# Convolution taps as one multiply-and-add per chunk, and new instruction orders in the second layer of a fused transformer kernel

## What is computed

```python
    h = _L0_tok_ref(x, L0_tok_w, L0_tok_b, L0_tok_cls_token, L0_tok_pos, 16)
    h = jnp.concatenate([h, txt], axis=1)
    h = h + _L0_attn_ref(_layernorm(h, axis=-1), ...)
    h = h + _L0_ffn_ref(_layernorm(h, axis=-1), ...)
    h = h + _L1_attn_ref(_layernorm(h, axis=-1), ...)
    h = h + _L1_ffn_ref(_layernorm(h, axis=-1), ...)
```

```python
        h = bit_linear(x, w1)                                    # 256 -> 1024, rounded to 8 bits
        h = depthwise_conv1d(h.transpose(0, 2, 1), conv_w, conv_b)   # 3 taps along the tokens
        h = h.transpose(0, 2, 1)
        h = jax.nn.silu(h)
        return bit_linear(h, w2)                                 # 1024 -> 256
```

## Time and profile before

| | |
|---|---|
| Median of 3 runs | 844.23 us (842.24 to 848.17) |
| The profiled execution | 845.46 us |
| its span, first to last instruction | 843.6 us |
| mean granted clock of TensorE | 0.952 |
| TensorE busy | 773.1 us (92%) |
| VectorE busy | 596.0 us (71%) |
| ScalarE busy | 440.7 us (52%) |
| GpSimd busy | 379.4 us (45%) |

### The profile page before, as it was taken

The page is one execution under the profiler, slowest core; times in us unless marked ns, Lnnn a source line. Parts: engine busy times, 40 slices in busy tenths (PEclk is TensorE's granted clock), DMA queues, the critical chain, the costliest instruction groups (busy, mean ns, idle before and its releaser), DMA issues.

```text
span 843.6 us, 21269 instructions
## 1 busy us (share of the span) xinstructions
PE 773.1 (92%) x7399; PEld 715.3 (85%) x7399; DVE 596.0 (71%) x1446; ACT 440.7 (52%) x1047; POOL 379.4 (45%) x515
## 2 busy tenths in 40 slices
PE   4999999999999975699998999999999999999674
PEld 4999999999999965699997988988888888888464
DVE  0467776777777763144331468899999999999994
ACT  1444455444445432122221657777777777776552
POOL 1434545545555442222214766466666666653100
PEclk8999999999999986699998999899999999999788
DMA  5325321100000214577730000000000000000000
GB/s 174 99 65 205 61 58 17 25 9 9 8 9 15 64 41 35 160 219 216 208 104 21 10 13 10 8 16 15 16 16 15 15 15 16 14 9 8 10 12 14
DMA packets 27442, 43.30 MB, mean 51 GB/s; under 512 B 10549, under 2 KB 21722, under 8 KB 26826
## 3 DMA queue, kind: packets, MB, share of 16 engines
q1 hardware_dynamic: 17930, 33.03, 14.6%
q0 software_dynamic: 5808, 5.63, 3.0%
q10 hardware_dynamic: 3600, 3.28, 1.1%
HBM read 34.04 MB, written 7.88 MB: 50 GB/s over the span
## 4 chain that ended last, share of the span: by engine, by line
PE 56%; DVE 25%; issue 11%; DMA 4%; ACT 2%; POOL 1%; SPq 1%; DVEq 0%; ACTq 0%; POOLq 0%
PE bank_h L1533 5%; PE bank_b L1495 4%; PE bank_e L1507 4%; PE bank_d L1533 4%; PE bank_f L1507 4%; PE bank_g L1518 4%; PE bank_e L1691 3%; PE bank_c L1544 3%; PE bank_f L1691 3%; PE bank_c L1703 3%; PE bank_c L1484 2%; PE bank_d L1703 2%; DVE diff L926 2%; PE bank_a L1484 2%; DVE w L1241 2%
## 5 line engine op out<-in xcount | busy, mean ns | idle before, releaser
L484 POOL TENSOR_TENSOR qbd<-qt,consts_f 128x560 f32<-128x560 f32 x128 | 163.0, 1279 | 184.5 <-PE bank_e L1507 95.8
L633 ACT ACTIVATE pt<-bank_g 69x448 f32<-69x448 f32 x128 | 69.4, 542 | 34.7 <-PE bank_h L1518 33.3
L627 ACT ACTIVATE prob<-diff 112x345 f32<-112x345 f32 x128 | 62.0, 485 | 39.1 <-DVE diff L926 39.1
L1533 PE MATMUL bank_h<-values,pt 69*69 69x68 f32 x1024 | 76.4, 229 | 2.5 <-ACT pt L642 2.5
L1533 PEld LDWEIGHTS bank_h<-values,pt 69*69 69x69 f32 x1024 | 71.8, 146 | 3.0 <-ACT pt L633 3.0
L1533 PEld LDWEIGHTS bank_d<-values,pt 69*69 69x69 f32 x1024 | 70.5, 142 | 2.2
L1507 PEld LDWEIGHTS bank_e<-kt,qbd 128*112 128x112 f32 x640 | 71.0, 178 | 1.4
L1533 PE MATMUL bank_d<-values,pt 69*69 69x68 f32 x1024 | 71.8, 226 | 0.0
L1518 PE MATMUL bank_g<-consts_f,prob 112*69 112x112 f32 x512 | 71.5, 262 | 0.0
L1507 PEld LDWEIGHTS bank_f<-kt,qbd 128*112 128x112 f32 x640 | 71.1, 178 | 0.0
L1507 PE MATMUL bank_e<-kt,qbd 128*112 128x69 f32 x640 | 70.9, 258 | 0.0
(11 more groups left out here) (205 smaller groups left out, 1938.7 us busy)
## 6 DMA issues: line engine op xcount, KB each, us to landing
w<-in_w SPq DMA_DIRECT2D x25, 512.0 KB, 4.1
w<-in_w SPq DMA_DIRECT2D x1, 4096.0 KB, 15.0
patches<-in_patches SPq DMA_DIRECT2D x16, 222.0 KB, 2.6
expert_results<-prob ACTq DMA_DIRECT2D x25, 128.0 KB
expert_rows<-x SPq DMA_DIRECT2D x16, 138.0 KB
out<-h SPq DMA_DIRECT2D x16, 138.0 KB
f_raw<-in_f SPq DMA_DIRECT2D x2, 1024.0 KB, 7.8
wqkv<-in_wqkv SPq DMA_DIRECT2D x2, 768.0 KB
```

The source lines that it names most:

```text
L484: pool.tensor_tensor(qbd[u % 2][:], q.broadcast_to([128, NG, HPB, QG]), head_mask.unsqueeze(1).unsqueeze(3).broadcast_to([128, NG, HPB, QG ...
L627: act.activation(prob[u % 2][:], diff[u % 2][:], ACT.Exp, scale=DH ** -0.5).then_inc(S["prob_made"], 1)
L633: act.activation(pt[u % 2][:, :, 0:4, :].rearrange("t h g q -> t g h q"), banks["g"][0:T, 0:4 * SR].rearrange("t (g h q) -> t g h q", g=4, ...
L1533: ins = mm(heads_out[b][:, hd * (DH + 1):(hd + 1 + AHEAD) * (DH + 1)], pt[u % 2][:, i, :, :].rearrange("k g q -> k (g q)")[:, 0:T], values ...
```

## The change

The four VectorE operations of the outer taps become sixteen: for each chunk, add_tap multiplies hs by the channel's weight and adds yc in one scalar_tensor_tensor, in place, on 2 x 68 elements; eight in add_left, eight in add_right. left_tap, right_tap and their buffers go. The first tap now waits for all middle taps. conv_added counts to 16 for each pair instead of 2. scale_hidden, which writes hs, waits for the right taps of the previous pair.

```diff
-    a=[("turn_x", 1), ("turn_o", 3), ("turn_x2", 4), ("k", 1)],
-    b=[("project", 3), ("ffn_out", 6), ("turn_max", 5), ("v", 1)],
-    c=[("q", 1), ("hidden0", 4), ("hidden3", 4)],
-    d=[("spread2", 6), ("attend0", 2), ("spread1", 4)],
-    e=[("scores2", 2), ("hidden1", 4), ("scores0", 1)],
-    f=[("scores1", 2), ("scores3", 2), ("hidden2", 4)],
-    g=[("turn_p0", 2), ("turn_p1", 2), ("turn_p2", 2), ("turn_p3", 2)],
-    h=[("turn_p0", 2), ("turn_p1", 2), ("turn_p2", 2), ("turn_p3", 2)],
-    i=[("attend1", 3)],
+    a=[("k", 1), ("turn_x", 0), ("turn_o", 2), ("turn_x2", 3)],
+    b=[("turn_max", 5), ("v", 1), ("project", 2), ("ffn_out", 5)],
+    c=[("hidden0", 4), ("hidden3", 4), ("q", 0)],
+    d=[("spread2", 5), ("attend0", 1), ("spread1", 3)],
+    e=[("hidden1", 4), ("scores0", 1), ("scores2", 1)],
+    f=[("hidden2", 4), ("scores1", 1), ("scores3", 1)],
+    g=[("turn_p3", 2), ("turn_p0", 1), ("turn_p1", 1), ("turn_p2", 1)],
+    h=[("turn_p3", 2), ("turn_p0", 1), ("turn_p1", 1), ("turn_p2", 1)],
+    i=[("attend1", 2)],
...
-        taps = [cut(4), cut(5)]
...
-        FN = ("quant_chain quantized scale1_made diag1_made spread1_made hidden_made conv_mid left_made right_made conv_added tanh_made "
+        FN = ("quant_chain quantized scale1_made diag1_made spread1_made hidden_made conv_mid conv_added tanh_made "
...
-                act.wait_ge(F["conv_added"], 2 * (p + 1))
+                act.wait_ge(F["conv_added"], 2 * HFC * (p + 1))
...
+                wait(dve, F["conv_added"], 2 * HFC * (p - 1) + HFC + j1)
...
-            tap_weight = lambda k: conv[:, :, k:k + 1].unsqueeze(3).broadcast_to([128, HFC, 2, T - 1])
-
-            def left_tap(p):
+            def add_tap(p, j, dst, src, k):
+                dve.scalar_tensor_tensor(yc[:, j, :, dst:dst + T - 1], hs[:, j, :, src:src + T - 1], conv[:, j, k:k + 1],
+                                         yc[:, j, :, dst:dst + T - 1], ALU.mult, ALU.add).then_inc(F["conv_added"], 1)
+
+            def add_left(p):
 
                 for g, bank in enumerate(HIDDEN_BANKS):
                     dve.wait_ge(BK[bank], read_after(order, bank, f"hidden{g}", p))
-                dve.tensor_tensor(taps[0][:, :, :, 1:T], hs[:, :, :, 0:T - 1], tap_weight(0), ALU.mult).then_inc(F["left_made"], 1)
-
-            def right_tap(p):
-
-                for g, bank in enumerate(HIDDEN_BANKS):
-                    dve.wait_ge(BK[bank], read_after(order, bank, f"hidden{g}", p))
-                dve.tensor_tensor(taps[1][:, :, :, 0:T - 1], hs[:, :, :, 1:T], tap_weight(2), ALU.mult).then_inc(F["right_made"], 1)
-
-            def add_left(p):
-
-                dve.wait_ge(F["left_made"], p + 1)
                 dve.wait_ge(F["conv_mid"], HFC * (p + 1))
-                dve.tensor_tensor(yc[:, :, :, 1:T], yc[:, :, :, 1:T], taps[0][:, :, :, 1:T], ALU.add).then_inc(F["conv_added"], 1)
+                for j in range(HFC):
+                    add_tap(p, j, 1, 0, 0)
 
             def add_right(p):
 
-                dve.wait_ge(F["right_made"], p + 1)
-                dve.wait_ge(F["conv_added"], 2 * p + 1)
-                dve.tensor_tensor(yc[:, :, :, 0:T - 1], yc[:, :, :, 0:T - 1], taps[1][:, :, :, 0:T - 1],
-                                  ALU.add).then_inc(F["conv_added"], 1)
+                dve.wait_ge(F["conv_added"], 2 * HFC * p + HFC)
+                for j in range(HFC):
+                    add_tap(p, j, 0, 1, 2)
```

More of the change, by code:

```diff
@@ new lines, in body1 @@
+                if live(s, 1, PAIRS):
+                    turn_p(s - 1, 0)
+                if live(s, 2, PAIRS):
+                    project(s - 2)
+                if live(s, 1, PAIRS):
+                    scores(s - 1, 3)
+                    turn_p(s - 1, 1)
+                if live(s, 3, PAIRS):
+                    turn_quantized(s - 3)
+                if live(s, 1, PAIRS):
+                    attend(s - 1, 0)
+                    attend(s - 1, 1)
+                    turn_p(s - 1, 2)
@@ L1857 @@
+                if live(s, 5, PAIRS):
+                    ffn_out(s - 5)
+                if live(s, 3, PAIRS):
+                    spread_scale1(s - 3)
+            steps(pe, PAIRS, 5, body1)
 class Columns:
```

243 lines of the change are left out of this document (111 added, 132 removed).

## The result

| | before | after |
|---|---|---|
| Median, beside each other | 844.74 us (4 runs, 842.24 to 848.17) | 853.37 us (4 runs, 851.70 to 854.61) |
| Ratio | | 1.0098, 95% interval 1.007 to 1.0126 |
| The profiled execution, its span | 845.46 us, 843.6 us | 851.7 us, 849.9 us |
| Mean granted clock of TensorE | 0.952 | 0.956 |
| VectorE busy, instructions | 596.0 us, 1446 | 598.1 us, 1638 |

The kernel became 1% slower. The forecast was 837 us with a range of 824 to 850, so the time lies outside, on the other side of no change.

The account below looks back on a forecast made before the run. VectorE was taken to set the second layer's pace, TensorE 3% behind. Savings of 4.9 us between second and last hidden_max and 1.8 in filling took 845.46 to 838.8, or 837 against the median; range 824 to 850.

Parts of the forecast that it names:

- The taps: VectorE's outer taps: sixteen operations at 0.268 us, 4.29 a pair, replace four costing 4.81.
- Rival (c): Taps on VectorE do not overlap, so the kernel gets slower: step 21.9, total 853 us; chance 0.15.
- The step: Second layer, hidden_max to hidden_max: 21.09 becomes 20.9 us, with VectorE waiting 0.3 ahead of add_ffn.
- TensorE's largest wait: On TensorE, the largest wait was expected ahead of values or turn_max; no size given.
- Steps that I cost at nothing: Second layer's ScalarE and GpSimd: their delays were priced at zero, with 3.7 and 7.8 us of slack in 20.
- Nothing else on VectorE is added: VectorE's step: only the taps' cost changes, 21.09 - 4.81 + 4.29 = 20.6 us.
- Second to last hidden_max: Second layer, second to last pair's hidden_max: 278.5 us falls to 273.6, 4.9 less.
- Its two terms: In that stretch: VectorE work falls by 6.9 and 1.5 us; waits of 2.7 and 0.8 are added.
- Filling: Start of the second layer, around 530 to 535: a slow-clock stretch gives back 1.8 us, open from 0 to 3.5.
- Tail: Behind the last hidden_max: unchanged.
- The sum: Whole kernel: 4.9 plus 1.8, so 6.7 us less.
- Rival (b): No gain: the step stays at 21.1 us through TensorE or a late tanh, total 841 to 846; chance 0.18.

Follow-up runs that it names:

- e2: The changed kernel with GpSimd's add_bias moved behind mix; 843.06 us, ratio 0.9982 to the kernel before.
- e12: The changed kernel with GpSimd's gathers issued ahead of the last spread_query; 843.66 us, ratio 0.9968 to the kernel before.
- e7: e2 with ffn_out moved ahead of the third turn_p on TensorE's list; 843.92 us, ratio 0.9986 to the kernel before.
- e8: e7 with 20 instead of 8 idle products ahead of turn_max for the last two pairs; 844.4 us.
- e9: e2 with 20 instead of 8 idle products ahead of turn_max for the last pair alone; 843.36 us.
- e5: The kernel before with only z_unscale moved behind stats2 on VectorE's list; 848.16 us, ratio 1.0039 to the kernel before.
- e3: The kernel before, its orders kept, with the new taps in the places of add_left and add_right; 876.29 us, ratio 1.0368.

## Why the prediction was wrong, point by point

**The taps: right.** 0.268 each was forecast, 0.27 measured in all runs of eight that GpSimd doesn't interrupt; the duration of one is 355 ns on average (0.34 to 0.36 forecast):

```profile
L1201 DVE SCALAR_TENSOR_TENSOR w<-w,conv 128x136 f32<-128x136 f32 x256 | 73.2, 355 | 0.0
```

Rival (c) named the right sign and nearly the right time, 853, by a mechanism that is not there: the taps do overlap. That it came near is luck. The prediction cites the Trainium skill, page "VectorE: DVE Perf Modes", section "The DRAIN you can't avoid", for that rival; the same section adds that a next operation which is not held starts earlier, and with that the starts of 0.27 and 1.20 agree.

**The step: right but for one line of the sum.** 20.9 with 0.3 of wait ahead of add_ffn was forecast; e2 shows 20.95 with 0.29, and 0.20 ahead of row_max, which I hadn't named; e12 shows 20.94. TensorE's largest wait is ahead of turn_max in both, up to 0.8, as named. In after the step is 21.71.

**The step that failed** is the sentence "ScalarE and GpSimd have 3.7 and 7.8 us of slack in 20", under "Steps that I cost at nothing", together with "Nothing else on VectorE is added". I read GpSimd's busy share as whether it would be late, and no wait of VectorE's in the steps is for it. I didn't ask what runs beside what, so z_unscale and gate_hidden stand in the sum at their lone prices, and the runs show 1.16 us a step more for the two. The rows of before could have told me: the earlier trace rows has GpSimd at 12.15 of 20, so for six tenths of the time VectorE has GpSimd beside it, and in the same trace spread_query takes 1.86 where it starts during gate_hidden and 1.14 where it doesn't:

```profile
552.30 1.14 POOL L484 TENSOR_TENSOR qbd<-qt,consts_f 128x560 f32<-128x560 f32 x1
...
567.84 1.86 POOL L484 TENSOR_TENSOR qbd<-qt,consts_f 128x560 f32<-128x560 f32 x1 [4.48 <-ACT qt L663]
```

In before that cost nothing, since it was GpSimd that waited, and GpSimd had time. The new lists turned it round. Per line, between the kernels' whole second layers, z_unscale has 13.2 us in after and 3.4 in e2, gate_hidden 22.5 and 20.8:

```profile
L563 POOL DMA_INDIRECT base<-expert_results,yrow_i x32 | 58.4, 1825 | 13.8 <-issue 7.0 <-DMA expert_results<-prob 6.0 <-PE bank_e L1498 0.8
L572 POOL TENSOR_TENSOR h<-h,base 69x512 f32<-69x512 f32 x15 | 25.7, 1714 | 20.0 <-ACT base L822 20.0
L1222 DVE SCALAR_TENSOR_TENSOR w<-w 128x1104 f32<-128x1104 f32 x16 | 22.5, 1405 | 0.3 <-ACT w L829 0.2
L1344 DVE TENSOR_SCALAR qs<-am,f_mean 69x2 f32<-69x2 f32 x16 | 13.2, 825 | 0.0
```

(lines of after: busy us, mean ns of one, idle before; one gather had a mean of 1233 ns and one mix 1261 in before). The 1.16 a step meets 0.3 of wait for ffn_out that it hides, and a little more: 21.71 - 20.95 = 0.76 is what is left. Over the ten steps between the first and the eleventh pair that is 7.6 (217.10 less 209.51); the first pair's second eight taps, stretched too (3.58 for the eight from 523.04), add 1.3. The medians, 853.37 and 843.06, are 10.3 apart; the 1.4 that are left are not traced to a place.

**Second to last hidden_max.** Forecast 4.9 less than before, e2 has 278.52 - 274.81 = 3.7 less. Its two terms can be checked by the busy time in that stretch, 274.43 in before and 265.69 in e2. The work fell by 8.7, where 6.9 + 1.5 = 8.4 was forecast (I had multiplied 14 by 0.49, the rounded step's gain; with the taps' own 4.81 - 4.29 = 0.52 it is 7.3 + 1.5 = 8.8); VectorE's idle time grew from 4.1 to 9.1, by 5.0, where 3.5 was forecast. I had also read before's idle time as 2.6 from three rows, when the stretch as a whole has 4.1.

**Filling: wrong.** I took 1.8 from the stretch at 530 with a granted clock of 0.63. That stretch is gone (the clock is 1.00 in 530 to 535 in after and e2), and the time from the first to the second hidden_max fell from 24.58 to 20.94 in e2. But the first one comes later by as much. From the start of TensorE's 96 idle products at the head of the layer (442.08 in before, 440.33 in e2) to the second hidden_max it is 108.0 in both. In the profiles of e7, e8, e9 and e12 it is 108.2 to 111.4, and in e5's, with before's orders, 109.4, so the gain is nothing and there may be a loss of one or two. The scatter goes in part with TensorE's clock in 455 to 475: e2 and e8 (108.0 and 108.2) were granted 0.94 and 0.93 there, e9, e7 and e12 (111.4, 110.4 and 110.1) 0.83, 0.80 and 0.74; but before, with 108.0, had 0.83 as well. In after it is 112.0 at 0.77, of which the stretched first taps and one step of 0.8 more are two. So of after's 2.7 up to the second hidden_max, one profile can't say how much is the change.

**Tail.** Forecast unchanged, measured 16.0 against 15.0. TensorE in after:

```profile
835.92 0.44 PE L1779 MATMUL bank_b<-consts_f,zmax 128*69 128x128 f32 x2 [2.76 <-DVE zmax L1228]
837.60 0.83 PE L1725 MATMUL bank_d<-diag,consts_f 69*128 69x138 f32 x2 [1.24 <-DVE diag L1338]
838.22 4.90 PE L1433 MATMUL bank_g<-consts_f 128*128 128x128 f32 x22
```

In before, the last pair had a pause of 1.11 there, ran the same spread in 0.50 and the 22 idle products in 2.62, and ffn_out started 8.1 after hidden_max did; here it starts 9.1 after. Behind the pause of 2.76 TensorE's granted clock in 834 to 843 is 0.63, so the lower level of 1.2 GHz for most of its work, and ffn_out has to wait for the idle products. In e9, where the pause was filled, the two took 0.50 and 2.62 again, and the tail is 15.1.

**The sum.** Had GpSimd kept clear, the kernel would be e2: -3.7 from the second to the last hidden_max, +1.2 in the tail, +1 to +2 in the filling, together about -1; the medians say -1.6. So the forecast of -6.7 had two faults: some ten microseconds of contention that it didn't see, and five of small terms, each too kind. Rival (b), no gain, is what the kernel becomes once the contention is gone.

## What to carry to other kernels

A moved or added VectorE operation of the kinds that were held here (tensor_scalar, tensor_tensor and scalar_tensor_tensor, all operands in SBUF) has to be laid beside GpSimd's list in time, however idle GpSimd is: it can wait there for a whole operation of GpSimd's, and the trace shows the wait as duration. So compare the longest and the median duration of each line with the shortest before reading idle times, and where a tiny operation takes a microsecond, look for the operation on the other engine that ends with it. Moving one entry of the idle engine's list gave back ten microseconds; merging operations only pays if the work that goes away was not filling a wait (e3).
